# Lower triangles of 2,048 Gram matrices: four rows to a partition in place of two

## The chip, the cores and the metric

One NeuronCore of a Trainium2 chip runs the whole kernel. The metric is the device time of one execution in microseconds (us). The kernel before takes 437.03 us in the median of three runs (436.17 to 438.0).

## The reference

```python
B, N, D = (1024, 64, 256)          # the input really has 2048 of them
Z = jnp.einsum('bnd,bmd->bnm', inputs, inputs)
li, lj = jnp.tril_indices(64, k=-1)
return Z[:, li, lj]                # 2048 x 2016, float32
```

The input is 2048 x 64 x 256 in float32 (134 MB), the output 2048 x 2016 (16.5 MB). For each of the 2,048 batches all 64 rows are multiplied with each other, and what lies below the diagonal is stored row after row: row i has i values, so it begins at column i(i-1)/2.

## The kernel before, in words

**Tiles.** A tile is 16 batches: two *sides* of eight. There are 128 tiles. A matmul contracts over partitions, so the 256 numbers of a row must be brought onto partitions: they are cut into eight *chunks* of 32, and VectorE's transposition works on 32 x 32 blocks. A *slot* is one batch in each of the four quadrants of 32 partitions; each side has two slots.

**Load** (SP, L138). `x_pairs` (L62) joins two rows into a run of 512 numbers, 2,048 bytes. A side's DMA brings 256 such runs: partition p gets one run of slot 0 and one of slot 1. Two DMAs of 512 KB make a tile, into one of eight x_in slots (`IN_RING`); the load of tile t waits until tile t-8 has been turned, and those of tiles 2 to 4 until the tile before has landed (`APART`). After the load of every eighth tile SP issues the stores of a finished group (`store_whole`, L149, DMAs at L145), after waiting for its packing.

**First turn** (VectorE, L203). One instruction of 2,048 elements a partition turns all 32 x 32 blocks of a tile. A block has 32 partitions (32 row pairs, one batch) by 32 numbers; turned, it gives 32 partitions (numbers of a chunk) by 32 row pairs, which are written two elements apart, so that first and second rows of the pairs interleave and the 64 rows of a batch stand in order in x_turned. There are three such buffers (`LAP`); turn t waits for its load and for the matmuls of tile t-3.

**Matmuls** (TensorE, L256). For each slot, each chunk, each quadrant g and each side, the 32 x 64 piece of x_turned is both weights and moving side, so that 64 x 64 products add up over the eight chunks in PSUM. Eight array tiles (four quadrants by two sides) work side by side; each quadrant has a bank. The program is a loop over laps of three tiles. PSUM has two sets of four banks, with three slots each: a set fills in one and a half tiles. TensorE waits for `kept[1]` ahead of the first slot of set 1 and for `kept[0]` two chunks before the lap's end.

**Keep** (ScalarE, L282). Copies a full set from PSUM to `products`, which gathers a group of eight tiles (64 batches a side). Set 0's copy starts when half the lap is multiplied (`half_multiplied`), set 1's when the lap is.

**Row turn** (VectorE, L219). Per group four instructions (`PIECES`) of 1,024 elements turn products so that batches come onto partitions and the 64 columns j into the free dimension; the first is issued after turn t = 8 x group + 11, the others two tiles apart.

**Packing.** ScalarE copies rows to packed_rows (`pack`: L111 for short rows, L117 for pairs of long ones), in quarter pieces behind each keep; GpSimd carries the second halves of long rows across partitions (L122). Both wait until the store of the group two before has landed. The last group is shared with VectorE (L122) and GpSimd (L111).

The order on each engine is that of the program: SP the loads and stores, VectorE the turns with a row turn after every second one, ScalarE keep then packing.

Of the kernel before, what the change touches and what calls it, by code (L numbers as in the profile page):

```python
# [7 lines left out]
PARTS = 128  # L8
# [11 lines left out]
def gram_lower_triangle(nc: bass.Bass, x: bass.AP, y: bass.AP):  # L20
    BATCHES, ROWS, DIM = x.shape
    PACKED = y.shape[1]
    JOINED = ROWS // BLOCK
    CHUNKS = DIM // BLOCK
    SLOTS = 2
# [12 lines left out]
    SETS = 2  # L38
    SET_SLOTS = LAP * SLOTS // SETS
# [4 lines left out]
    GROUP_SLOTS = GROUP_TILES * SLOTS  # L44
# [16 lines left out]

    x_pairs = x.rearrange("b (i r) d -> (b i) (r d)", r=JOINED)  # L62

    with ExitStack() as stack:  # L64
# [5 lines left out]

        x_in = sbuf("x_in", [PARTS, IN_RING, SIDES * SLOTS, JOINED * DIM])
        x_turned = sbuf("x_turned", [PARTS, LAP, SIDES * SLOTS, CHUNKS, ROWS])
# [14 lines left out]
        half_multiplied = semaphore("half_multiplied")  # L87
# [9 lines left out]
        def place(t):  # L97

            return divmod(t + BLANK, LAP)

# [25 lines left out]
        def _(sync):  # L126
            def load(t):
# [67 lines left out]
        def _(dve):  # L195
            def turn(t):


                k, (lap, j) = t % IN_RING, place(t)
                dve.wait_ge(loaded[k], (t // IN_RING + 1) * (SIDES * 16))  # L200
                if lap > 0:
                    dve.wait_ge(tile_multiplied[j], lap * ARRAY_TILES)  # L202
                nc.vector.transpose(  # L203
                    x_turned[:, j].rearrange("p k c (i r) -> p k r c i", r=JOINED),
                    x_in[:, k].rearrange("p k (r c d) -> p k r c d", r=JOINED, c=CHUNKS)).then_inc(turned[j], LAP)

            def turn_rows(n):
                group, piece = divmod(n, PIECES)
                rows = piece_rows(piece)
                if piece == 0:  # L210

                    lap, s = divmod(((group + 1) * GROUP_SLOTS - 1 + BLANK * SLOTS) // SET_SLOTS, SETS)
                    dve.wait_ge(kept[s], (lap + 1 + s) * LAP)
                if group > 0:
# [5 lines left out]
                    row_halves[:, rows].rearrange("p i h j -> p (i h) j"),  # L220
# [20 lines left out]
        def _(pe):  # L241
            def multiply(j, step):

                pe.wait_ge(turned[j], step)
                for slot in range(SLOTS):
                    s, at = divmod(j * SLOTS + slot, SET_SLOTS)
                    if s == 1 and at == 0:
                        pe.wait_ge(kept[1], step)
                    for c in range(CHUNKS):
# [3 lines left out]
                        for g in range(QUADRANTS):  # L253
                            for side in range(SIDES):
                                rows = x_turned[g * BLOCK:(g + 1) * BLOCK, j, side * SLOTS + slot, c, :]
                                done = nc.tensor.matmul(  # L256
                                    bank_sets[s][side * HALF:(side + 1) * HALF, g, at, :], rows, rows,
                                    start=c == 0, stop=c == CHUNKS - 1)
                                if c == CHUNKS - 1:
                                    if slot == SLOTS - 1:  # L260
                                        done.then_inc(tile_multiplied[j], 1)
                                    elif at == SET_SLOTS - 1:
                                        done.then_inc(half_multiplied, 1)
# [6 lines left out]
        def _(act):  # L270
            def keep(lap, s):

                act.wait_ge(half_multiplied if s == 0 else tile_multiplied[LAP - 1], (lap + 1) * ARRAY_TILES)
                begin = (lap * SETS + s) * SET_SLOTS - BLANK * SLOTS
                slot, end = max(0, begin), begin + SET_SLOTS
                while slot < end:
                    group, in_group = divmod(slot, GROUP_SLOTS)
                    count = min(end - slot, GROUP_SLOTS - in_group)
                    if group >= KEPT_RING and in_group == 0:
# [3 lines left out]
                        products[:, group % KEPT_RING, :, in_group * QUADRANTS:(in_group + count) * QUADRANTS].rearrange(  # L283
# [47 lines left out]
```

## Time and profile before

| | |
|---|---|
| median of 3 runs | 437.03 us |
| profiled execution | 437.67 us, span 435.9 us |
| granted TensorE clock, mean | 0.975 |
| PE, PE weight loads | 88%, 87% of the span busy |
| DVE, ACT, POOL | 83%, 41%, 45% |
| load and store queue | 95.3% of 16 engines' span |
| HBM read, written | 134.22 MB, 16.52 MB, mean 346 GB/s |

The span runs from the first to the last instruction; the execution's own time is 1.8 us longer. PE is TensorE, DVE VectorE, ACT ScalarE, POOL GpSimd, SPq the queue of SyncE. Busy shares are means over the span. "issue" is time in which an engine waited for nothing that the profile shows. The granted clock is given as a share of 2.4 GHz, TensorE's upper level (the lower is 1.2 GHz).

### The profile page before, as it was taken

How to read it: one execution, taken by the hardware profiler on the slowest of the kernel's cores; microseconds unless marked ns; L12 is line 12 of the kernel's file. 1: busy time of each engine (PE TensorE's matmuls, PEld its weight loads, DVE VectorE, ACT ScalarE, POOL GpSimd, SP SyncE). 2: the span in 40 equal slices, each digit the busy share in tenths (PEclk: the TensorE clock that was granted, in tenths of full speed). 3: DMA queues.
4: the chain of work that ended last, by engine and by line, in shares of the span. 5: the costliest groups of instructions: out<-in, count | busy, mean ns of one | idle time of the engine just before them, and what ended most of it. 6: DMA issues, size and time to landing. Idle time of an engine off the chain costs nothing.

```text
span 435.9 us, 68822 instructions
## 1 busy us (share of the span) xinstructions
PE 385.4 (88%) x33024; PEld 377.5 (87%) x33024; DVE 363.7 (83%) x224; ACT 179.3 (41%) x834; POOL 197.2 (45%) x980
## 2 busy tenths in 40 slices
PE   4569999999999999999998999989899998989810
PEld 4569999999999999999998989989899998989810
DVE  5248899999999999897997979799697979979734
ACT  0101125454444535354444544533445454345372
POOL 0000082745628174471817446281744628173584
PEclk9999999999999999999999999999899999999965
DMA  5589999999999999999999999999999999999416
GB/s 199 192 312 388 387 387 387 387 391 392 387 398 386 402 387 368 369 394 357 356 398 344 390 377 387 353 352 378 373 384 368 379 365 373 361 386 368 107 34 156
DMA packets 72378, 151.01 MB, mean 346 GB/s; under 512 B 4640, under 2 KB 4768, under 8 KB 72352
## 3 DMA queue, kind: packets, MB, share of 16 engines
q1 hardware_dynamic: 72352, 150.75, 95.3%
q14 instruction: 20, 0.16, 0.1%
q8 instruction: 6, 0.10, 0.1%
HBM read 134.22 MB, written 16.52 MB: 346 GB/s over the span
## 4 chain that ended last, share of the span: by engine, by line
PE 35%; DMA 28%; DVE 16%; SPq 10%; issue 6%; POOL 3%; ACT 0%; DVEq 0%; POOLq 0%
PE bank_set L256 35%; DMA x_in<-x_dram 25%; DVE x_turned L203 12%; SPq L138 9%; DVE row_halves L219 3%; DMA y_dram<-packed_rows 3%; POOL packed_rows L122 3%; DVE packed_rows L122 1%; DVE x_turned L225 0%; SPq L145 0%; ACT packed_rows L117 0%; ACT products L282 0%; DVEq L202 0%; DVEq L218 0%; DVEq L64 0%
## 5 line engine op out<-in xcount | busy, mean ns | idle before, releaser
L256 PE MATMUL bank_set<-x_turned 32*64 32x64 f32 x33024 | 385.4, 237 | 30.0 <-issue 12.1
L256 PEld LDWEIGHTS bank_set<-x_turned 32*64 32x64 f32 x33024 | 377.5, 132 | 37.8 <-issue 21.9
L203 DVE STREAM_TRANSPOSE x_turned<-x_in 128x2048 f32<-128x2048 f32 x128 | 290.6, 2286 | 58.0 <-DMA x_in<-x_dram 41.5
L122 POOL COPY packed_rows<-row_halves 32x60 f32<-32x60 f32 (+30 forms) x961 | 194.9, 204 | 232.3 <-DMA y_dram<-packed_rows 132.5
L282 ACT COPY products<-bank_set 128x768 f32<-128x768 f32 (+2 forms) x96 | 69.0, 729 | 215.4 <-PE bank_set L256 204.9
L219 DVE STREAM_TRANSPOSE row_halves<-products 128x1024 f32<-128x1024 f32 x64 | 76.8, 1203 | 6.9 <-POOL packed_rows L122 5.0
L117 ACT COPY packed_rows<-row_halves 128x128 f32<-128x128 f32 x256 | 56.4, 300 | 17.4 <-DMA y_dram<-packed_rows 15.9
L111 ACT COPY packed_rows<-row_halves 128x32 f32<-128x32 f32 (+30 forms) x481 | 62.3, 220 | 0.0
L282 ACT ACT_TABLE_LOAD x1 | 1.3, 1283 | 15.8 <-PE bank_set L256 15.8
L122 DVE COPY packed_rows<-row_halves 32x2 f32<-32x2 f32 (+30 forms) x31 | 3.5, 191 | 0.0
L225 DVE MEMSET x_turned<- 128x2048 f32 x1 | 1.8, 1765 | 1.2 <-PEq L325 1.2
L111 POOL COPY packed_rows<-row_halves 128x2 f32<-128x2 f32 (+14 forms) x15 | 2.1, 195 | 0.1
L325 POOL MEMSET const-float32-0.0<- 128x1 f32 x1 | 0.1, 99 | 0.2 <-issue 0.2
L325 POOL MEMSET const-bfloat16-1.0<- 128x1 bf16 x1 | 0.1, 102 | 0.0
L325 POOL MEMSET const-uint8-127<- 128x1 uint8 x1 | 0.1, 102 | 0.0
L325 POOL MEMSET const-float32-1.0<- 128x1 f32 x1 | 0.1, 99 | 0.0
## 6 DMA issues: line engine op xcount, KB each, us to landing
x_in<-x_dram SPq DMA_DIRECT2D x256, 512.0 KB, 10.8
y_dram<-packed_rows SPq DMA_DIRECT2D x30, 504.0 KB, 9.6
y_dram<-packed_rows SPq DMA_DIRECT2D x2, 380.0 KB, 3.9
y_dram<-packed_rows SPq DMA_DIRECT2D x2, 124.0 KB, 3.9
```

Of the source, the lines that this page charges most:

```text
L111: return copy(packed_rows[:, group % 2, :, at:at + i], row_halves[:, i, :, 0:i])
L117: return copy(two[:, :, :, 0:BLOCK], row_halves[:, i:i + 2].rearrange("p w h j -> p h w j"))
L122: return copy(packed_rows[first:first + BLOCK, group % 2, :, at + BLOCK:at + i], row_halves[first + BLOCK:first + HALF, i, :, 0:i - BLOCK])
L138: sync.dma_start(x_in[:, k, side * SLOTS:(side + 1) * SLOTS], x_pairs[first:first + PER_SIDE * BLOCK].rearrange("(k p) e -> p k e", p=PART ...
L203: nc.vector.transpose(x_turned[:, j].rearrange("p k c (i r) -> p k r c i", r=JOINED), x_in[:, k].rearrange("p k (r c d) -> p k r c d", r=J ...
L219: nc.vector.transpose(row_halves[:, rows].rearrange("p i h j -> p (i h) j"), products[:, group % KEPT_RING, rows, :].rearrange("p i (h q) ...
L225: nc.vector.memset(x_turned[:, j], 0.0).then_inc(turned[j], LAP)
L256: done = nc.tensor.matmul(bank_sets[s][side * HALF:(side + 1) * HALF, g, at, :], rows, rows, start=c == 0, stop=c == CHUNKS - 1)
L282: last = nc.scalar.copy(products[:, group % KEPT_RING, :, in_group * QUADRANTS:(in_group + count) * QUADRANTS].rearrange("p i (m g) -> p i ...
L325: nc = bacc.Bacc("TRN2", target_bir_lowering=False, num_devices=1)
```

## The change

A run becomes four rows (1,024 numbers, 4,096 bytes), so a side's DMA is 128 runs, one per partition, and 32 partitions hold two batches of 16 runs. A row's number is 4i + r in run i; with i = 8h + n and r = 2u + v it is 32h + 4n + 2u + v. The first turn writes each turned block (32 columns: two batches of 16 runs) so that the rows of a batch stand in the order (h, u, n, v). The matmul takes this order as weights, so the products' partitions have it; on the moving side and in its output the columns are walked so that the products' columns come out in true order: the 64 results of a matmul go to PSUM in pairs of neighbours, four elements apart. The row turn puts the remaining order of the other index right: it writes pairs (v) of neighbours, four elements apart (n), for each u.

PSUM's two sets now hold two tiles and one tile: the keep of set 0 starts when the second tile of a lap is multiplied, and its copy has 1,024 elements, that of set 1 512. The copies' patterns get a dimension more (quadrant and slot change places). ScalarE's packing behind the two keeps is four and two quarter pieces a lap in place of three and three.

```diff
-    JOINED = ROWS // BLOCK
+    JOINED = 4
+    PAIR = 2
+    PAIRS = JOINED // PAIR
-    SLOTS = 2
+    SLOTS = BLOCK * JOINED // ROWS
-    SETS = 2
-    SET_SLOTS = LAP * SLOTS // SETS
+    SET_TILES = (2, 1)
+    SETS = len(SET_TILES)
...
-        x_in = sbuf("x_in", [PARTS, IN_RING, SIDES * SLOTS, JOINED * DIM])
-        x_turned = sbuf("x_turned", [PARTS, LAP, SIDES * SLOTS, CHUNKS, ROWS])
+        x_in = sbuf("x_in", [PARTS, IN_RING, SIDES, JOINED * DIM])
+        x_turned = sbuf("x_turned", [PARTS, LAP, SIDES, CHUNKS, SLOTS, ROWS])
...
+        def set_of(j):
+            return (0, j) if j < SET_TILES[0] else (1, j - SET_TILES[0])
...
-                    first = (group * GROUP + side * KEPT + in_group * PER_SIDE) * BLOCK
-                    sync.dma_start(x_in[:, k, side * SLOTS:(side + 1) * SLOTS],
-                                   x_pairs[first:first + PER_SIDE * BLOCK].rearrange("(k p) e -> p k e", p=PARTS)
-                                   ).then_inc(loaded[k], 16)
+                    first = (group * GROUP + side * KEPT) * (ROWS // JOINED) + in_group * PARTS
+                    sync.dma_start(x_in[:, k, side], x_joined[first:first + PARTS]).then_inc(loaded[k], 16)
...
                 nc.vector.transpose(
-                    x_turned[:, j].rearrange("p k c (i r) -> p k r c i", r=JOINED),
-                    x_in[:, k].rearrange("p k (r c d) -> p k r c d", r=JOINED, c=CHUNKS)).then_inc(turned[j], LAP)
+                    x_turned[:, j].rearrange("p s c b (h u n v) -> p u v (s c b h) n", h=ROWS // BLOCK, u=PAIRS, v=PAIR),
+                    x_in[:, k].rearrange("p s (u v e) -> p (u v) s e", u=PAIRS, v=PAIR)).then_inc(turned[j], LAP)
...
                 nc.vector.transpose(
-                    row_halves[:, rows].rearrange("p i h j -> p (i h) j"),
+                    row_halves[:, rows].rearrange("p i h (n u v) -> p (i h) u n v", u=PAIRS, v=PAIR),
...
-                                rows = x_turned[g * BLOCK:(g + 1) * BLOCK, j, side * SLOTS + slot, c, :]
+                                rows = x_turned[g * BLOCK:(g + 1) * BLOCK, j, side, c, slot]
                                 done = nc.tensor.matmul(
-                                    bank_sets[s][side * HALF:(side + 1) * HALF, g, at, :], rows, rows,
+                                    bank_sets[s][side * HALF:(side + 1) * HALF, g, at, :].rearrange(
+                                        "r (n u v) -> r u n v", u=PAIRS, v=PAIR),
+                                    rows,
+                                    rows.rearrange("d (h u e) -> d u h e", h=ROWS // BLOCK, u=PAIRS),
                                     start=c == 0, stop=c == CHUNKS - 1)
...
-                act.wait_ge(half_multiplied if s == 0 else tile_multiplied[LAP - 1], (lap + 1) * ARRAY_TILES)
+                j = SET_TILES[0] * s
+                act.wait_ge(tile_multiplied[j + SET_TILES[s] - 1], (lap + 1) * ARRAY_TILES)
...
-                        products[:, group % KEPT_RING, :, in_group * QUADRANTS:(in_group + count) * QUADRANTS].rearrange(
-                            "p i (m g) -> p i m g", g=QUADRANTS),
-                        bank_sets[s][:, :, slot - begin:slot - begin + count, :].rearrange("p g m i -> p i m g"))
+                        products[:, group % KEPT_RING, :, in_group * PER_SIDE:(in_group + count) * PER_SIDE].rearrange(
+                            "p i (m g b) -> p i m g b", g=QUADRANTS, b=SLOTS),
+                        bank_sets[s][:, :, (t - begin) * SLOTS:(t - begin + count) * SLOTS, :].rearrange(
+                            "p g (m b) i -> p i m g b", b=SLOTS))
...
-                    while n + PACK_LAG < (lap * SETS + s + 1) * SET_SLOTS - BLANK * SLOTS:
+                    while n + PACK_LAG < (lap * LAP + (SET_TILES[0] if s == 0 else LAP) - BLANK) * 2:
```

## Rows read from the trace of the kernel before

**Rows 1.** The page: span, busy time, load queue, bytes.

```profile
span 435.9 us, 68822 instructions
PE 385.4 (88%) x33024; PEld 377.5 (87%) x33024; DVE 363.7 (83%) x224; ACT 179.3 (41%) x834; POOL 197.2 (45%) x980
...
q1 hardware_dynamic: 72352, 150.75, 95.3%
...
HBM read 134.22 MB, written 16.52 MB: 346 GB/s over the span
```

**Rows 2.** The chain of waits in order of time: start us, us, what.

```profile
27.83 10.45 PE bank_set L256 x475
...
56.25 8.78 PE bank_set L256 x423
...
163.05 6.12 PE bank_set L256 x296
169.30 2.32 DVE x_turned L203
171.62 0.24 SPq L138
171.90 12.72 DMA x_in<-x_dram
```

**Rows 3.** Three stretches: length, busy us (instructions) of PE, PEld, DVE, ACT, POOL, clock, DMA, GB/s.

```profile
27.80:169.20 141.40, 139.52 (x12095) 137.52 (x12096) 128.83 (x67) 56.73 (x243) 63.35 (x310) 1.00 1.05 389
169.20:415.50 246.30, 232.93 (x20206) 227.98 (x20199) 215.66 (x117) 110.26 (x523) 120.73 (x589) 0.99 0.99 358
...
36.00:60.00 24.00, 23.59 (x2094) 23.20 (x2082) 20.53 (x11) 4.00 (x5) 4.97 (x24) 1.00 1.05 387
```

**Rows 4.** The waits: who for whom, us in total, times, longest us.

```profile
DVE x_turned L203 <- DMA x_in<-x_dram: 41.5, 15, 4.2
...
ACT packed_rows L117 <- DMA y_dram<-packed_rows: 15.9, 9, 3.6
```

**Rows 5.** The timeline of the end: start us, us, engine, line [idle before <- releaser].

```profile
407.54 20.07 POOL L122 COPY packed_rows<-row_halves 32x32 f32<-32x32 f32 x93 [10.22 <-DMA y_dram<-packed_rows]
...
412.50 2.95 PE L256 MATMUL bank_set<-x_turned 32*64 32x64 f32 x256 [1.05 <-DVE x_turned L203]
...
417.21 3.79 ACT L111 COPY packed_rows<-row_halves 128x32 f32<-128x32 f32 x31
...
422.81 3.50 DVE L219 STREAM_TRANSPOSE row_halves<-products 128x1024 f32<-128x1024 f32 x3 [5.01 <-POOL packed_rows L122]
...
426.34 3.49 DVE L122 COPY packed_rows<-row_halves 32x2 f32<-32x2 f32 x31
```

**Rows 6.** What the DMA engines moved, in 40 slices: 30 to 60 us, then 160 to 200.

```profile
GB/s 410 401 399 407 396 391 388 385 391 385 388 382 391 391 382 391 385 388 385 390 382 388 388 388 388 382 391 385 385 385 391 388 388 388 385 388 382 390 391 385
...
GB/s 391 381 383 391 377 387 391 383 414 401 352 314 307 350 307 295 356 377 397 401 408 389 381 371 373 365 391 395 389 383 385 391 387 385 449 408 319 239 334 358
```

**Rows 7.** Line 138, the issue of loads on SP: durations in ns, time to landing.

```profile
L138 SPq DMA_DIRECT2D x_in<-x_dram x256: 368/1229/3982, 0.7 to 397.3; - x128
...
DMA to landing us min/median/max: 3.3/10.8/15.2
```

**Rows 8.** Groups by form: count, busy us, mean ns, idle before by releaser.

```profile
L203 DVE STREAM_TRANSPOSE x_turned<-x_in 128x2048 f32<-128x2048 f32 x128 | 290.6, 2286 | 58.0 <-DMA x_in<-x_dram 41.5 <-PE bank_set L256 16.5
L219 DVE STREAM_TRANSPOSE row_halves<-products 128x1024 f32<-128x1024 f32 x64 | 76.8, 1203 | 6.9 <-POOL packed_rows L122 5.0 <-ACT products L282 1.9
L282 ACT COPY products<-bank_set 128x768 f32<-128x768 f32 x75 | 60.0, 800 | 185.1 <-PE bank_set L256 174.6 <-issue 10.4
...
L282 ACT COPY products<-bank_set 128x512 f32<-128x512 f32 x10 | 5.9, 589 | 18.1 <-PE bank_set L256 18.1
...
L111 ACT COPY packed_rows<-row_halves 128x32 f32<-128x32 f32 x16 | 3.6, 223 | 0.0
```

**Rows 9.** The timeline of the start, TensorE.

```profile
9.89 2.35 PE L256 MATMUL bank_set<-x_turned 32*64 32x64 f32 x128 [3.14 <-issue]
```

More of the change, by code:

```diff
@@ L59, in gram_lower_triangle @@
     STORES = SIDES * 16
-    x_pairs = x.rearrange("b (i r) d -> (b i) (r d)", r=JOINED)
+    x_joined = x.rearrange("b (i r) d -> (b i) (r d)", r=JOINED)
     with ExitStack() as stack:
@@ L210, in turn_rows @@
                 if piece == 0:
-                    lap, s = divmod(((group + 1) * GROUP_SLOTS - 1 + BLANK * SLOTS) // SET_SLOTS, SETS)
+                    lap, j = place((group + 1) * GROUP_TILES - 1)
+                    s = set_of(j)[0]
                     dve.wait_ge(kept[s], (lap + 1 + s) * LAP)
@@ L244, in multiply @@
                 pe.wait_ge(turned[j], step)
+                s, in_set = set_of(j)
+                if s == 1 and in_set == 0:
+                    pe.wait_ge(kept[1], step)
                 for slot in range(SLOTS):
-                    s, at = divmod(j * SLOTS + slot, SET_SLOTS)
-                    if s == 1 and at == 0:
-                        pe.wait_ge(kept[1], step)
+                    at = in_set * SLOTS + slot
                     for c in range(CHUNKS):
@@ L254, in multiply @@
                             for side in range(SIDES):
-                                rows = x_turned[g * BLOCK:(g + 1) * BLOCK, j, side * SLOTS + slot, c, :]
+                                rows = x_turned[g * BLOCK:(g + 1) * BLOCK, j, side, c, slot]
                                 done = nc.tensor.matmul(
-                                    bank_sets[s][side * HALF:(side + 1) * HALF, g, at, :], rows, rows,
+                                    bank_sets[s][side * HALF:(side + 1) * HALF, g, at, :].rearrange(
+                                        "r (n u v) -> r u n v", u=PAIRS, v=PAIR),
+                                    rows,
+                                    rows.rearrange("d (h u e) -> d u h e", h=ROWS // BLOCK, u=PAIRS),
                                     start=c == 0, stop=c == CHUNKS - 1)
[L259 to L263, printed above, removed]
+                                if c == CHUNKS - 1 and slot == SLOTS - 1:
+                                    done.then_inc(tile_multiplied[j], 1)
             with pe.Fori(LAP, (LAPS + 1) * LAP, LAP) as step:
@@ L271, in keep @@
             def keep(lap, s):
-                act.wait_ge(half_multiplied if s == 0 else tile_multiplied[LAP - 1], (lap + 1) * ARRAY_TILES)
[L274 to L278, printed above, removed]
+                j = SET_TILES[0] * s
+                act.wait_ge(tile_multiplied[j + SET_TILES[s] - 1], (lap + 1) * ARRAY_TILES)
+                begin = lap * LAP + j - BLANK
+                t, end = max(0, begin), begin + SET_TILES[s]
+                while t < end:
+                    group, in_group = divmod(t, GROUP_TILES)
+                    count = min(end - t, GROUP_TILES - in_group)
                     if group >= KEPT_RING and in_group == 0:
```

4 lines of the change are left out of this document (1 added, 3 removed).

## The prediction

> **What bounds the kernel now.** I read the page first: a span of 435.9 us in an execution of 437.67 us, TensorE busy for 88% of it, VectorE for 83%, the load queue for 95% [rows 1]. Three resources are near full, so the averages decide nothing and the stage does. The chain in order of time shows two stages [rows 2]. From 56.25 to 163.05 us it is TensorE alone, twelve laps of three tiles in 106.8 us, 8.90 us a lap or 2.967 us a tile. From 169.3 us on it goes through the load, the issue of loads on SP and the first turn (L203). The split by stretch says the same [rows 3]: up to 169.2 us TensorE is busy 139.5 of 141.4 us, after it 232.9 of 246.3 us, with 13.4 us idle. The waits name the giver: L203 waited 41.5 us for loads [rows 4]. So two thirds of the kernel wait for loads that come a little too slowly.
>
> How much too slowly: TensorE's second lap starts at 27.83 us [rows 2] with 126 tiles to go. By 169.2 us it has done 141.4 / 2.967 = 47.6 of them; the other 78.4 take until 415.45 us [rows 5], 3.14 us each. A tile's loads are 512 packets of 2,048 bytes, 1.049 MB, at the 387 GB/s of the stretch without stores 2.71 us [rows 3]; the other 0.43 us are the share of stores (0.13 MB a tile) and hold-ups. The queue thus falls behind by 3.14 - 2.967 = 0.173 us a tile from the start, and what it had in hand (eight x_in slots) covers 47.6 x 0.173 = 8.2 us. Check: 126 x 0.173 - 8.2 = 13.6 us, the idle time seen.
>
> **The change part by part.**
>
> *Loads.* The 134.22 MB read [rows 1] come in runs of 2,048 bytes, 65,536 packets; now in 32,768 of 4,096; bytes, DMAs (256) and their order stay. The trace has no load in 4,096-byte packets. Lower bound of the gain: none, 2.71 us a tile. Upper bound: the best slice of the trace, 449 GB/s in the stretch from 160 us, where a store lies beside loads: 2.34 us. I take the row nearest to a pure load at its best, the first four slices after 30 us (410, 401, 399, 407 GB/s, mean 404) [rows 6]: 2.60 us. Then a tile costs the queue 3.03 us, the lag is 0.063 us a tile, 126 x 0.063 = 7.9 us, inside the 8.2 us in hand: TensorE never waits. So 13.6 us go. A rate of 404 GB/s is also the point from which they go entirely; at 395 GB/s (2.65 us) 126 x 0.113 - 8.2 = 6.0 us would stay.
>
> A load stream in rows of 4 KiB issued from SP is given 408.7 GB/s in the Trainium skill (DMA: Bandwidth & Descriptors, iDMA fabric). By it a tile's loads would cost 2.57 us and the sum would be the same; no run here shows it yet.
>
> *Issues on SP.* A load's issue lasts 1.2 us in the median and lands 10.8 us later, 256 packets each [rows 7]: SP is held back by a full queue, with some eight DMAs out. With half the packets it can run further ahead, until x_in slots hold it. The store sits behind the load of the same tile as before. SP then comes to a store some tiles earlier and may wait there for ScalarE's packing with loads behind it; that is hidden by what is already queued, and without that cover costs the same lag as above. No direct term.
>
> *First turn (L203).* 128 instructions of 2,048 elements, before 2.286 us [rows 8], output in steps of 8 bytes over runs of 32; now in steps of 8 bytes over runs of 8, then a jump. *Row turn (L219).* 64 instructions of 1,024 elements at 1.203 us with an output without steps; now pairs of elements 16 bytes apart. The two rows differ by 1.08 us for 1,024 elements, 1.06 ns each, and L219 alone is at 1.17 with its fixed part: the 8-byte step costs nothing today. I take both unchanged. Bounds: nothing, or the price of a stall at each jump, which no row shows; what can be said is the room: 2.286 + 1.203 / 2 = 2.89 us a tile against 2.967, or 2.7%. Up to that it is hidden by TensorE.
>
> *Matmuls.* Their number stays, 33,024. The weights are read as before; the moving side reads runs of 16 elements, and the 64 results land in pairs of 8 bytes, 16 bytes apart. Eight array tiles run side by side, so each takes a weight load and a matmul in 2.967 / 32 = 92.7 ns. Lower bound: nothing changes; upper: one cycle of the 2.4 GHz level (granted clock 1.00) lost at each of 32 pairs, 13 ns, 14%. I take nothing, as nearest to the only row there is, L203's steps being free on its own port.
>
> The rule that speaks against this part is in the Trainium skill (PSUM — Partial Sum Buffer, Specifications): PSUM lines are of 8 bytes, and "any non-contiguous AP slows matmuls significantly". Advanced Engine Details and Errata, Memory Cachelines, is milder: every two consecutive elements should be contiguous, which pairs keep. By the first the third rival below comes true; by the second the sum stands. The trace cannot say, since every output in it is contiguous.
>
> *Keeps on ScalarE (L282).* Before, two copies of 768 elements a lap, 0.800 us each; now one of 1,024 and one of 512. By the forms of 512 and 768 at 0.589 and 0.800 us [rows 8] the first is 1.01 us: 1.60 us a lap both ways. What moves is the due time. The set of two tiles is free for reading after two thirds of a lap instead of half, and TensorE asks for it at 14/16 of the third tile: 14/16 x 2.967 = 2.60 us for a copy of 1.01 us, 1.3 us to spare with the start delay. Behind a keep ScalarE packs: now four quarter pieces after the large one and two after the small (three and three before). Four short ones are 16 copies of 0.22 us, 3.5 us [rows 8]: with the keep 4.5 us after two thirds of the lap, so that the small keep starts 1.5 us late, but TensorE needs its set only two thirds of a lap (5.9 us) on. Two are 1.8 us, done long before the large keep is due. Its waits for stores came to 15.9 us in nine [rows 4]; one of over 4 us after the small keep would reach TensorE. The longest was 3.6 us, so no cost.
>
> *Head.* Up to 27.83 us TensorE works in chunks of 128 matmuls with gaps that no engine releases, as the 3.14 us before the one at 9.89 us [rows 9]; the loads of tiles 2 to 4 are still issued one by one. Unchanged; 1 us either way.
>
> *Tail.* Today the last matmul ends at 412.50 + 2.95 = 415.45 us and the span 20.45 us later. In it, the last group's row turns wait 5.0 us for GpSimd at 422.81 us: its 62 carries of the group before start only at 407.54 us, after 10.22 us of waiting for a store that lands behind queued loads [rows 5]. With loads ahead of TensorE that store lands well before and this wait goes. Next in line is ScalarE, which must free the rows: 31 short copies ended at 421.0 us, 5.55 us after the last matmul. From there one row turn (1.2 us), VectorE's 31 carries (3.49 us) and the final stores (429.83 to 435.9, 6.1 us): 16.3 us. If the store lands no earlier than the last load must (393 us), GpSimd ends at 408.5 and the tail is some 19.7 us.
>
> **Sum.** 27.83 + 126 x 2.967 (373.8) = 401.7 us for the last matmul, + 16.3 = 418.0 us of span, + 1.8 us around it = 419.8 us, against 437.67 us. The median of the runs before, 437.03, lies 0.6 us under the profiled one, so I predict 419.5 us, 4% less.
>
> **The rivals.**
> 1. *A packet of 4,096 bytes moves no faster* (or is cut in two by the queue, so the change does nothing). For: the rate rests at 387 GB/s for 24 us with all engines at work, whatever the packet's fixed part. Then 13.6 us of idle time and the old tail stay: 437 us. Between this and the forecast lie 388 to 404 GB/s, 425 to 434 us.
> 2. *VectorE becomes the bound.* Its turns would have to lengthen by over 2.7% to show, and by (13.6 + 4.1) / 126 = 0.14 us a tile more, so 7.5%, to eat the whole gain. At 15%, 2.89 becomes 3.32 us a tile: 27.8 + 418.6 + 16.3 + 1.8 = 464 us. Against: steps of 8 bytes are free in L203's row.
> 3. *The matmuls slow down at their results' pairs.* TensorE is the very engine that is left as the bound, so each per cent costs 3.7 us; break-even at 17.7 / 373.8 = 4.7%. At one cycle a pair, 3.38 us a tile: 27.8 + 426 + 16.3 + 1.8 = 472 us. For: nothing in the trace has such an output. Against: moving and writing go on in other array tiles meanwhile.
>
> **How the numbers follow.** Forecast (414 to 425 us) 0.60; part of the loads' wait stays (425 to 434) 0.13; rival 1, 0.09; rival 2, 0.06; rival 3, 0.12. A measurement of this kernel can tell some 0.5% from no change. So faster 0.73, same 0.09, slower 0.18. The range runs from 414 us (head and tail each somewhat shorter) to 437 us, rival 1's own time, leaving rivals 2 and 3 out.
>
> **What would show it.** Right: load packets 32,768 and the queue at 400 GB/s or more in the steady stretch; laps of 8.90 us up to the last one; L203 waiting for TensorE, not for loads; L203 at 2.28 us, L219 at 1.20 us; the large keep at 1.01 us; the last matmul near 402 us and no wait for GpSimd in the tail. Wrong: a lap above 9.0 us with TensorE busy throughout (rival 3, matmul rows longer), VectorE at 9 tenths everywhere with TensorE waiting for it and no load wait (rival 2), 387 GB/s again (rival 1).

## The result and the profile after

The changed kernel takes 429.87 us in the median of four runs (429.42 to 430.58), the kernel before 437.45 us beside it: ratio 0.983, 95% interval 0.981 to 0.985. It is faster, by 1.7%, where 4% were forecast (419.5 us), and it stands inside the stated range, 414 to 437 us.

The page of the profiled execution (430.24 us), to be laid beside [rows 1]:

```profile
span 428.5 us, 68861 instructions
PE 379.3 (89%) x33024; PEld 372.2 (87%) x33024; DVE 365.0 (85%) x224; ACT 177.9 (42%) x829; POOL 197.3 (46%) x980
...
DMA packets 39610, 151.01 MB, mean 352 GB/s; under 512 B 4640, under 2 KB 4768, under 8 KB 39584
...
q1 hardware_dynamic: 39584, 150.75, 92.8%
```

The 32,768 packets fewer are there, and TensorE is busy for 6.1 us less. That already is a surprise, since its instructions are as many as before. The chain in order of time shows three stages (start us, us, what):

```profile
21.90 4.22 issue
26.12 2.27 PE bank_set L264 x114
28.39 4.47 issue
32.86 10.62 PE bank_set L264 x512
...
61.28 8.66 PE bank_set L264 x431
...
316.42 8.67 PE bank_set L264 x433
...
331.33 1.01 ACT products L291
...
382.52 17.53 DMA y_dram<-packed_rows
400.10 0.20 POOL packed_rows L130
```

TensorE's second lap starts at 32.86 us, 5.03 us later than in [rows 2]. From 61.28 to 316.42 us lie 29 laps, 8.80 us each against 8.90. From 331 us on it waits for loads again, and a store of 17.53 us leads into the tail. The timeline gives the end (start us, us, engine, line, last the idle time before and who ended it):

```profile
400.10 20.07 POOL L130 COPY packed_rows<-row_halves 32x32 f32<-32x32 f32 x93 [9.41 <-DMA y_dram<-packed_rows]
...
404.99 2.95 PE L264 MATMUL bank_set<-x_turned 32*64 32x64 f32 x256 [0.73 <-DVE x_turned L208]
...
415.37 3.50 DVE L225 STREAM_TRANSPOSE row_halves<-products 128x1024 f32<-128x1024 f32 x3 [5.29 <-POOL packed_rows L130]
```

The last matmul ends at 407.94 us and the span 20.6 us after it, the same tail as in [rows 5]: GpSimd starts its last 62 carries when the store lands, and the last group's row turns wait for it for 5.29 us. The groups by form answer to [rows 8]:

```profile
L208 DVE STREAM_TRANSPOSE x_turned<-x_in 128x2048 f32<-128x2048 f32 x128 | 292.0, 2290 | 49.2 <-PE bank_set L264 29.5 <-DMA x_in<-x_dram 18.7
L225 DVE STREAM_TRANSPOSE row_halves<-products 128x1024 f32<-128x1024 f32 x64 | 76.9, 1205 | 6.9 <-POOL packed_rows L130 5.3 <-ACT products L291 1.6
...
L291 ACT COPY products<-bank_set 128x1024 f32<-128x1024 f32 x37 | 37.5, 1012 | 164.2 <-PE bank_set L264 146.2 <-issue 18.0
L291 ACT COPY products<-bank_set 128x512 f32<-128x512 f32 x54 | 31.1, 586 | 47.7 <-PE bank_set L264 46.3 <-issue 1.1
```

The new patterns cost VectorE nothing to speak of: 2,290 ns against 2,286, and 1,205 against 1,203. The large keep takes 1,012 ns.

**Where the time went.** I split each span into the same parts: start of the second lap, 42 laps at the steady rate, what TensorE waits beyond that, and the tail after the last matmul. The third term is a remainder. It holds more than waits for loads: the second lap is longer than the steady ones in every kernel, by 1.7 us before (27.83 to 38.41 us) and by 2.0 us after (32.86 to 43.70 us). That leaves 12.1 and 3.6 us for loads that come late.

| us | second lap | 42 laps (one) | waits | last matmul ends | tail | span |
|---|---|---|---|---|---|---|
| before | 27.8 | 373.8 (8.90) | 13.8 | 415.4 | 20.5 | 435.9 |
| forecast | 27.8 | 373.8 (8.90) | 0 | 401.7 | 16.3 | 418.0 |
| after | 32.9 | 369.5 (8.80) | 5.6 | 407.9 | 20.6 | 428.5 |

Between the two kernels the span falls by 7.4 us: 8.2 us of waits and 4.3 us of laps are won, 5.0 us of head are lost. The forecast missed by 10.5 us: +5.0 in the head, -4.3 in the laps, +5.6 in the waits, +4.3 in the tail.

### The profile page after: what moved, and what is told of

Its sections match the earlier page's. It is cut to its first block, busy times and chain, and to the rows that moved or that the text cites. A ratio compares the mean times of both kernels' runs of the same rounds, so it can differ in the third digit from the quotient of the medians.

```text
span 428.5 us, 68861 instructions
## 1 busy us (share of the span) xinstructions
PE 379.3 (89%) x33024; PEld 372.2 (87%) x33024; DVE 365.0 (85%) x224; ACT 177.9 (42%) x829; POOL 197.3 (46%) x980
## 4 chain that ended last, share of the span: by engine, by line
PE 72%; SPq 11%; issue 6%; DMA 4%; POOL 3%; DVE 2%; ACT 0%; DVEq 0%; POOLq 0%; ACTq 0%
PE bank_set L264 72%; SPq L146 10%; DMA y_dram<-packed_rows 4%; POOL packed_rows L130 3%; SPq L151 1%; DVE packed_rows L130 1%; DVE row_halves L225 1%; DVE x_turned L231 0%; ACT products L291 0%; ACT packed_rows L125 0%; DVEq L67 0%; SPq L157 0%; DVEq L224 0%; POOLq L187 0%; ACTq L282 0%
## 5 line engine op out<-in xcount | busy, mean ns | idle before, releaser
L264 PE MATMUL bank_set<-x_turned 32*64 32x64 f32 x33024 | 379.3, 236 | 28.7 <-issue 18.2
L264 PEld LDWEIGHTS bank_set<-x_turned 32*64 32x64 f32 x33024 | 372.2, 132 | 35.6 <-issue 28.1
L208 DVE STREAM_TRANSPOSE x_turned<-x_in 128x2048 f32<-128x2048 f32 x128 | 292.0, 2290 | 49.2 <-PE bank_set L264 29.5
L291 ACT COPY products<-bank_set 128x512 f32<-128x512 f32 (+1 forms) x91 | 68.6, 759 | 211.9 <-PE bank_set L264 192.5
L225 DVE STREAM_TRANSPOSE row_halves<-products 128x1024 f32<-128x1024 f32 x64 | 76.9, 1205 | 6.9 <-POOL packed_rows L130 5.3
L291 ACT ACT_TABLE_LOAD x1 | 1.3, 1283 | 20.6 <-PE bank_set L264 20.6
```

The lines of the kernel that those rows point to most:

```text
L208: nc.vector.transpose(x_turned[:, j].rearrange("p s c b (h u n v) -> p u v (s c b h) n", h=ROWS // BLOCK, u=PAIRS, v=PAIR), x_in[:, k].rea ...
L225: nc.vector.transpose(row_halves[:, rows].rearrange("p i h (n u v) -> p (i h) u n v", u=PAIRS, v=PAIR), products[:, group % KEPT_RING, row ...
L264: done = nc.tensor.matmul(bank_sets[s][side * HALF:(side + 1) * HALF, g, at, :].rearrange("r (n u v) -> r u n v", u=PAIRS, v=PAIR), rows, ...
L291: last = nc.scalar.copy(products[:, group % KEPT_RING, :, in_group * PER_SIDE:(in_group + count) * PER_SIDE].rearrange("p i (m g b) -> p i ...
```

## The experiments

"Second lap", "waits" and "tail" are the parts of the table above, read from the one execution of each kernel that was traced, and totals are medians of two to ten executions. The runs before beside the experiments lie at 436.8 to 437.2 us.

### The sets alone, on the kernel before

```diff
# on the kernel before
-    SET_SLOTS = LAP * SLOTS // SETS
+    SET_TILES = (2, 1)
...
-                                if c == CHUNKS - 1:
-                                    if slot == SLOTS - 1:
-                                        done.then_inc(tile_multiplied[j], 1)
-                                    elif at == SET_SLOTS - 1:
-                                        done.then_inc(half_multiplied, 1)
+                                if c == CHUNKS - 1 and slot == SLOTS - 1:
+                                    done.then_inc(tile_multiplied[j], 1)
```

(with ScalarE's trigger, its packing and the waits of TensorE as in the change; two-row loads and all patterns stay)

> The kernel before with PSUM sets of two tiles and one tile and nothing else of the change: two-row loads, one increment-group (half_multiplied) gone, no wait inside a tile. Theory (the lap fell from 8.90 to 8.79 us because the accounting of the sets changed, not the patterns): steady laps of 8.79 us, head and packets as before, the waits for loads begin a little earlier since TensorE asks sooner, so the time falls by 0 to 2 us only. Rival (the lap fell because of the new patterns of operands or results): laps stay at 8.90 us and the time is that of before within 0.3%.

Measured: 436.95 us, ratio 1.001 (0.999 to 1.003). The chain in order of time of this kernel:

```profile
28.93 3.93 issue
32.87 10.31 PE bank_set L260 x489
...
43.31 8.64 PE bank_set L260 x430
51.95 0.12 issue
52.08 8.65 PE bank_set L260 x426
```

Laps of 8.77 us: the shorter lap belongs to the sets, not to the new patterns. The patterns themselves cost at most 0.03 us a lap, and probably nothing, since the kernels with small stores and with stores from ScalarE (below) have the new patterns and laps of 8.77 us too. What I had not expected is the first number: the second lap starts at 32.87 us, as in the changed kernel, with packets of 2,048 bytes. So the head's 5 us do not need the larger packets. My expectation of the head "as before" was wrong. The two cancel: 42 x 0.13 = 5.5 us gained, 5.0 lost.

This run is also the clean partner of the changed kernel: same sets, same head (32.87 and 32.86 us), two DMAs a tile in both. What differs is the row layout with its packets of 4,096 bytes: 436.95 against 429.87 us, 7.1 us. They come out of the waits: 12.9 us here (last matmul at 414.19 us), 5.6 after; without the longer second lap 11.2 and 3.6 us.

### Eight increments a lap put back

```diff
# on the changed kernel
                                 if c == CHUNKS - 1 and slot == SLOTS - 1:
                                     done.then_inc(tile_multiplied[j], 1)
+                                elif c == CHUNKS - 1 and j == 1:
+                                    done.then_inc(half_multiplied, 1)
```

> The changed kernel with eight more semaphore increments a lap on the last matmuls of the first slot of the second tile, which nobody waits for. Theory (the lap fell by 0.11 to 0.13 us with the sets because eight increments a lap went with them): laps of 8.90 us again, 4.6 us more in all up to where loads bound. Rival (it fell because TensorE's wait for the second set no longer stands inside a tile): laps stay at 8.79 us.

Measured: 430.21 us (427.54 to 432.55), 0.3 us more than the changed kernel, where up to 4.6 us were expected. The execution traced is the slowest, 432.55 us. The timeline of TensorE shows nine laps in 80.29 us:

```profile
124.11 80.12 PE L265 MATMUL bank_set<-x_turned 32*64 32x64 f32 x6912 [0.17 <-issue]
204.39 80.12 PE L265 MATMUL bank_set<-x_turned 32*64 32x64 f32 x6912 [0.17 <-issue]
```

8.92 us a lap: an increment on a matmul costs TensorE some 15 ns. Against the changed kernel's trace (430.24 us) 42 x 0.12 = 5.0 us are lost in the laps, and 2.7 are given back, since the waits fall from 5.6 to 2.9 us as TensorE comes later. That is the 2.3 us between the two traced executions; the medians differ by less, within the 5 us over which this kernel's four runs scatter.

### Two increments a tile in place of eight

On the kernel with stores from ScalarE and spaced loads (below), only the last quadrant's two matmuls tell that a tile is done.

```diff
-    ARRAY_TILES = QUADRANTS * SIDES
+    ARRAY_TILES = SIDES
...
-                                if c == CHUNKS - 1 and slot == SLOTS - 1:
+                                if c == CHUNKS - 1 and slot == SLOTS - 1 and g == QUADRANTS - 1:
```

> The kernel with stores from ScalarE's queue and spaced loads, and only the matmuls of the last quadrant (two in place of eight) telling that a tile is done, so 6 increments a lap in place of 24. The run with 8 more increments had laps of 8.91 us against 8.79, so 15 to 16 ns each. Theory (each increment costs TensorE its 15 ns): 18 fewer take 0.27 us off a lap, 8.50 us. The loads then bound: the queue's 24.7 us a group of eight tiles is 3.09 us a tile against 2.83, so TensorE waits from the middle on and the total falls by 0 to 3 us only, 416.5 to 420 us. Rival (only the increments inside a tile cost, those at a tile's end lie beside a wait): laps stay at 8.77 us.

Measured: 420.17 us, no gain on its base (419.5). The laps fell from the base's 8.77 to 8.50 us as computed, 11.3 us in all, and the second lap starts 1.1 us sooner, at 28.76 us. The waits took all of it: 16.8 us against 3.8. At this point the loads are the bound, and a faster TensorE gains nothing.

### Packets of 2,048 bytes in the changed kernel, and four DMAs in the kernel before

```diff
# on the changed kernel; the waits for a tile's loads count 32 a side in place of 16
-                    sync.dma_start(x_in[:, k, side], x_joined[first:first + PARTS]).then_inc(loaded[k], 16)
+                    for half in range(2):
+                        part = slice(half * 2 * DIM, (half + 1) * 2 * DIM)
+                        sync.dma_start(x_in[:, k, side, part], x_joined[first:first + PARTS, part]).then_inc(
+                            loaded[k], 16)
```

> The changed kernel with each load cut in two along the run, so that all packets are of 2,048 bytes again (four DMAs of 256 KB a tile) while turns, matmuls and sets stay changed. Theory (the packets give the queue its rate, and their number in the queue sets both the run-ahead of SP and the head): queue at 387 GB/s, packet 84 ns, TensorE's second lap starts near 28 us as before instead of 32.9, laps of 8.79 us while fed, waits for loads from some 160 us on, total 435 to 438 us. Rival A (the head comes from the order and spacing of the loads, not from the packets): second lap still starts at 32 to 33 us and the total is 440 us or more. Rival B (the gain is TensorE's shorter lap alone): total stays at 430 us.

Measured: 443.81 us, ratio 1.016 (1.011 to 1.020), slower than the kernel before. The second lap starts at 29.9 us. Neither expectation fits: the total is above the theory's 435 to 438 us, and the head is shorter than rival A's 32 to 33 us. The edit also doubles the DMAs, so a second run does that alone, on the kernel with the sets alone:

```diff
-                    sync.dma_start(x_in[:, k, side * SLOTS:(side + 1) * SLOTS],
-                                   x_pairs[first:first + PER_SIDE * BLOCK].rearrange("(k p) e -> p k e", p=PARTS)
-                                   ).then_inc(loaded[k], 16)
+                    for slot in range(SLOTS):
+                        at = first + slot * PARTS
+                        sync.dma_start(x_in[:, k, side * SLOTS + slot], x_pairs[at:at + PARTS]).then_inc(loaded[k], 16)
```

> The kernel before with sets of two tiles and one (two-row loads) and each load cut by slot into two DMAs of 128 packets: four DMAs of 256 KB a tile, packets of 2,048 bytes, as in the run of the changed kernel with packets of 2,048 bytes. It tells how much of that run's 443.8 us is the number of DMAs. Theory (half is the packets, half the DMAs): 440 to 444 us, as there. Rival (the number of DMAs costs nothing, the packets all): 437 us, as with two DMAs a tile.

Measured: 441.48 us, 4.5 us over the two-DMA kernel. Four DMAs of 256 KB a tile are dearer than two of 512 KB with the same packets. The 2.3 us by which the changed kernel so cut (443.81 us) still lies above this one are not explained. Two views say what the packets do. DMA, 36 to 60 us, of the changed kernel cut to 2,048 bytes, then of the changed kernel with spaced loads (below), which streams undisturbed there:

```profile
DMA packets 5093, 9.29 MB, mean 387 GB/s; under 512 B 566, under 2 KB 566, under 8 KB 5092
```

```profile
DMA packets 2712, 9.89 MB, mean 412 GB/s; under 512 B 300, under 2 KB 300, under 8 KB 2711
```

The larger packet is worth 6% of the rate; it gives more than the 404 GB/s that I had taken. The Trainium skill's 408.7 GB/s for rows of 4 KiB (DMA: Bandwidth & Descriptors, iDMA fabric) agrees with the 412 within 1%. While TensorE bounds, the changed kernel itself shows no such rate (380 GB/s from 36 to 60 us): SP waits there for free x_in slots.

### More loads spaced

```diff
# on the changed kernel, and likewise on the kernel before with the sets alone
-    APART = range(2, 5)
+    APART = range(2, 7)
```

> The changed kernel with the loads of tiles 2 to 6 issued one by one instead of tiles 2 to 4. Theory (the two gaps of 4.2 and 4.5 us in TensorE's first lap are fetches of its program that stand behind loads which now run further ahead): the gaps fall to 2.2 to 3 us, the second lap starts at 28.5 to 30 us, but the waits for loads of the end stay or grow, since two loads come later; total 427 to 429.5 us. Rival (the gaps come from the size of the packets alone): second lap at 32.9 us again and a total at or above 430 us.

> The kernel before with sets of two tiles and one and the loads of tiles 2 to 6 issued one by one, packets of 2,048 bytes. Theory (the head's delay of 5 us belongs to the moment at which the unspaced loads are released, not to the packet size): second lap at 29 to 30 us instead of 32.9 us; the total stays within 1.5 us of 437 us, since loads bound from the second half on. Rival: head unchanged.

Measured: the changed kernel falls to 426.0 us (0.977, 0.972 to 0.982), 1 us below the range that I gave, since the waits did not grow (4.7 us). The kernel before with the sets alone rises to 439.85 us, a miss: I had it within 1.5 us of 437. The changed kernel's chain now reads

```profile
25.03 2.27 PE bank_set L264 x115
27.31 2.28 issue
29.59 10.16 PE bank_set L264 x475
```

The gaps of 4.2 and 4.5 us are 2.6 and 2.3 us, and the second lap starts at 29.59 us. In the other kernel it starts at 27.93 us, 4.9 us earlier, and the total is 2.9 us worse. The reason is in the waits, 21.4 us against 12.9: with spaced loads the DMA engines move 252 GB/s from 30 to 36 us in place of 393 and 209 in place of 265 before that, and TensorE waits for loads from 115 us on. I read this as the queue's idle time in the head, which a kernel that the queue bounds does not get back.

What decides the head? TensorE runs 128 matmuls, then waits with no engine to release it; the instruction queue of the page has six packets, 0.10 MB, one for each 128 of a lap's 768 matmuls. SP's own waits show when the free loads are let go. Where three loads are spaced, the sum of SP's waits for them and the start of the second lap are: before 16.8 us and 27.8; stores from ScalarE 15.8 and 28.5, on the kernel before 15.8 and 30.3; packets cut 14.7 and 29.9; more increments 14.2 and 32.9; sets alone 14.1 and 32.9; small stores 13.8 and 32.3; after 13.6 and 32.9. Longer waits of SP mostly go with an earlier second lap, but the sets alone with four DMAs break the rule: 12.1 and 28.8. The two views of SP's waits, before and after:

```profile
SPq L138 <- DMA x_in<-x_dram: 16.8, 3, 6.6
```

```profile
SPq L146 <- DMA x_in<-x_dram: 13.6, 3, 6.0
```

In the changed kernel the flood of unspaced loads starts 3 us earlier, and two gaps are over 4 us where the kernel before has none. I read this as fetches of TensorE's program that stand beside the loads. That the fetch is what TensorE waits for is inferred. The granted clock is no rival: it is 0.66 in the first 30 us of the kernel with the sets alone and 1.00 in the kernels before and after, and the steps of 128 matmuls take 2.25 to 2.36 us in all three. Why the sets let the spaced loads land sooner stays open. So does whether it is the sets: moving the stores to ScalarE changes no instruction of this stretch on SP or TensorE, and it shortens the changed kernel's head by 4.4 us and lengthens that of the kernel before by 2.5. The head shifts by several us with edits elsewhere.

### Small stores

```diff
# on the changed kernel
             def store_whole(group):
...
-                store(group, slice(0, PACKED))
+                store(group, slice(0, 128))
```

This leaves out columns 128 to 2,015 of the output of all groups but the last.

> The changed kernel with the stores of all groups but the last cut to their first 128 columns; the other columns of these groups are left out of the output. Theory (stores cost the queue 4.3 us a group, by holding some engines back, and that is why TensorE waits for loads from 331 us on and why the last store lands 17.5 us after its issue): no wait of TensorE for the first turn after the head, the last matmul at 32.9 + 42 x 8.79 = 402 us, GpSimd's wait in the tail gone, total 418 to 421 us. Rival (loads alone at 412 GB/s with eight slots are late): waits stay and the total is above 425 us.

Measured: 420.1 us in the median of two runs; last matmul at 402.28 us, tail 15.7 us. TensorE waits for no turn after the head; the waits' whole list for L208 is

```profile
DVE x_turned L208 <- PE bank_set L264: 31.7, 47, 10.2
...
DVE x_turned L208 <- DMA x_in<-x_dram: 5.9, 3, 2.4
```

So the loads of the changed kernel are late because of the stores, and so is the tail. In the stretch where loads bound, eight tiles of the changed kernel take 24.8 and 24.6 us (the same matmul of three successive groups starts at 355.62, 380.41 and 404.99 us). Its loads need 8 x 1.049 MB / 412 GB/s = 20.4 us, which leaves 4.3 us for two stores; I had carried over 8 x 0.43 = 3.4 us.

### Stores from ScalarE's queue

```diff
# on the changed kernel; SP keeps the stores of the last two groups
             def pack(n):
...
                 if quarter == 3:
                     last.then_inc(packed_home, 1)
+                if piece == 0 and quarter == 3 and 0 < group < GROUPS - 1:
+                    done = group - 1
+                    act.wait_ge(packed_home, (done + 1) * PIECES)
+                    act.wait_ge(packed_across, (done + 1) * LONG_PIECES)
+                    for side in range(SIDES):
+                        first_row = done * GROUP + side * KEPT
+                        nc.scalar.dma_start(y[first_row:first_row + KEPT, :].rearrange("(h q) c -> q h c", q=BLOCK),
+                                            packed_rows[side * HALF:side * HALF + BLOCK, done % 2, :, :]).then_inc(
+                            stored[done % 2], 16)
```

> The changed kernel with the stores of groups 0 to 13 issued from ScalarE's queue instead of SP's, each after the first long quarter pieces of the next group. Theory (the tail is long because the store of group 12 stands behind loads in SP's queue: 17.5 us from issue to landing, so GpSimd begins its last 62 carries only at 400.1 us; the loads are late because stores take engine time, whatever queue they come from): a store lands in under 9 us, GpSimd's and ScalarE's waits for stores shrink, the part after the last matmul falls from 20.6 to 16 to 17 us, while the waits of the first turn for loads stay within 2 us of those of the changed kernel (18.7 us); total 424 to 427 us. Rival (the stores delay by standing in line, not by engine time): the waits for loads vanish too, total at or below 421 us.

Measured: 419.84 us, 0.961 (0.959 to 0.964) of the kernel before and 10 us under the changed kernel. The total is below the first theory's 424 to 427 us and in the rival's range (at or below 421); the parts decide between them. The timeline of GpSimd at the end:

```profile
388.08 15.27 POOL L130 COPY packed_rows<-row_halves 32x32 f32<-32x32 f32 x62 [8.95 <-DVE row_halves L221]
405.34 5.13 POOL L130 COPY packed_rows<-row_halves 32x32 f32<-32x32 f32 x31 [1.99 <-DMA y_dram<-packed_rows]
```

The last 62 carries start at 388.08 us, released by VectorE's row turn and no longer by a store. The tail is 15.3 us. That store was issued at 372.62 us in place of 381.48, and no store from ScalarE took over 9.4 us to land, against 18.5 from SP: it is issued sooner as well as landing sooner, and these runs do not part the two. The waits stay at 5.2 us, so the mechanism is the first theory's: they do not vanish with the stores out of SP's queue. Of the 11.3 us that the span is shorter, 5.3 are the tail, 4.4 the head, 28.48 us here, which neither theory had, 1.2 the laps (8.77 us) and 0.4 the waits. The two together,

> Both together: stores from ScalarE's queue and the loads of tiles 2 to 6 issued one by one. If the two gains are independent: head as in the run with spaced loads (second lap at 29.6 us), tail of 16 to 17 us, total 420 to 423 us. Rival (an earlier TensorE meets the same late loads, so the head's gain is lost to them): total as with the stores alone.

give 419.5 us (0.961, 0.958 to 0.964): second lap 29.85 us, waits 3.8, last matmul 401.86 us against 401.92 with the stores alone. The rival holds: by then the head no longer counts. Against the changed kernel with spaced loads alone (426.0 us), whose head is within 0.3 us of this one's, moving the stores is worth 6.5 us, 5.2 of them in the tail; the waits fall by 0.9 us only. And on the kernel before, with its own sets and packets:

> The kernel before with the stores of groups 0 to 13 issued from ScalarE's queue. Theory (the tail's 4 to 5 us are a matter of the store's place behind loads, in both kernels): the part after the last matmul falls from 20.5 to 15.5 to 16.5 us, the waits for loads stay, total 431 to 434 us. Rival (the shorter tail needs the faster loads): 436 to 438 us.

432.01 us (0.990, 0.986 to 0.993), tail 16.1 us. The store's place in SP's queue cost both kernels over 4 us.

### What holds the queue back at the end

DMA of the changed kernel with stores from ScalarE and spaced loads, 376 to 402 us in 40 slices; its last loads are in it:

```profile
DMA  9999999999930000000000000000000000000999
GB/s 426 399 449 381 418 412 409 403 410 410 372 126 25 25 25 25 32 25 25 25 25 25 32 25 25 25 25 13 0 0 0 0 0 0 0 0 0 198 198 198
```

For some 10 us the queue moves 25 GB/s, a sixteenth of its rate. I read this as one DMA engine still at work when fifteen are done, with the last load landing when it is. With small stores this stretch is missing. Three runs on this base ask what puts it behind.

```diff
# stores by half: 32 packets a DMA in place of 64, two DMAs for one
+                        for h in range(RUNS):
+                            at = done * GROUP + side * KEPT + h * BLOCK
+                            nc.scalar.dma_start(y[at:at + BLOCK, :],
+                                                packed_rows[side * HALF:side * HALF + BLOCK, done % 2, h, :]).then_inc(
+                                stored[done % 2], 16)
# more instructions on SP, after each load from tile 8 on
+                    for extra in range(20):
+                        sync.wait_ge(turned[extra % LAP], 1)
# more instructions on GpSimd, after each piece of groups 0 to 12
+                        for extra in range(80):
+                            pool.wait_ge(turned[extra % LAP], 1)
```

> The kernel with stores from ScalarE's queue and spaced loads, each store cut into its two halves of 32 batches: 32 packets of 8,064 bytes a DMA in place of 64. In the run before this cut, one DMA engine alone was still at work (25 GB/s) for some 10 us after the others had emptied their last loads. Theory S (the stores' spread over the engines or their clash there puts that engine behind): the lone engine's stretch changes by over 3 us either way and the total with it. Theory F (it also carries the instruction fetches, 0.26 MB, which at 25 GB/s are 10 us): the stretch stays at 9 to 11 us, total 419 to 422 us, more DMAs costing 0 to 2 us.

> The same base with 2,400 more instructions on SP that wait for nothing (semaphores long reached), some 150 KB of program at 64 bytes each, or about 19 fetches of 8 KB. Theory F (one engine carries all fetches and each load's landing waits for it): the lone engine's stretch at the end grows from 10 us to 14 to 17 us, TensorE's waits for loads begin earlier and grow, total 3 to 6 us more than 419.5. Theory S: stretch 9 to 11 us, total 419 to 421 us.

> The run with more instructions on SP became 7 us longer, but SP also issues the loads. Here some 1,040 empty instructions (80 waits a piece, merged in pairs) stand on GpSimd instead, behind its carries of groups 0 to 12, where it has 9 us a group to spare and issues no load. Theory F (fetches delay the loads): some 8 fetches more, TensorE's waits for the first turn grow from 3.8 to 8 or 9 us, total 423 to 426 us. Rival (the run on SP was longer because SP issued its loads later): waits as in the base, total 419 to 421 us.

Stores by half: 421.62 us and the same lone stretch. Halving the stores' packets a DMA does not matter. More instructions on SP: 427.35 us, waits 9.9 us, above the 3 to 6 us more that were forecast; on GpSimd: 421.04 us, waits 5.3 us against 3.8, not the 8 or 9 forecast. The page counts the fetches of the run on GpSimd:

```profile
q14 instruction: 29, 0.24, 0.1%
q8 instruction: 6, 0.10, 0.1%
```

Eight fetches of 8 KB more than its base's 21 cost 1.5 us, inside the scatter of the runs (419.7 to 422.5 against 417.8 to 422.6). The run on SP got less than it was meant to: the 2,400 waits became 1,200 instructions and 9 fetches more, not 19. What tests the theory of the fetches best is the lone stretch. At 25 GB/s nine more fetches would lengthen it by some 3 us (an estimate from these counts), but 25 GB/s last 9 to 10 us in the two kernels with more fetches as in their base. I therefore read most of what the run on SP lost as SP's own delay in issuing loads, which no run shows by itself. That a sixteenth of the queue ends late is shown, and that without the stores' bytes it does not. The two runs with more fetches speak against the fetches, and what in the stores does it stays open.

## Why the prediction was right or wrong

**Direction, bound and main cause held.** The gain of the row layout comes, as the prediction had it, from TensorE's waits for loads: 12.9 us fall to 5.6 between the two kernels that differ in it alone. Turns, matmul patterns and keeps cost what was taken: 2,290 and 1,205 ns, at most 0.03 us a lap, 1,012 ns. It is luck that the total misses by no more than 10.5 us: the laps, which I had as unchanged, gave 4.3 us that hide as much of the three other misses. Rival 1 fell (412 GB/s), rival 2 fell, and rival 3 with it: results in pairs of 8 bytes do not slow a matmul down. On the Trainium skill's two sentences (PSUM — Partial Sum Buffer, Specifications, and Advanced Engine Details and Errata, Memory Cachelines), this trace agrees with the milder one for pairs, though the section that has it repeats the strict one beside it; no run here has other patterns.

**"Then a tile costs the queue 3.03 us ... TensorE never waits"** failed. The rate term was too low (412 against 404 GB/s, 2.55 us a tile), but the term for stores and hold-ups was 0.54 us a tile, not the 0.43 carried over: 3.09 us. And TensorE asked sooner, every 2.93 us. By 331 us the lag of 0.16 us a tile had used up what was in hand, and 3.6 us of waits for loads stayed.

The account of what was in hand was wrong too, and there it was luck that the miss is not larger: 126 x 0.16 - 8.2 would be 12 us of waits. The lag does not run "from the start". The first stores are issued at 90.0 us before and 91.6 us after, and until then a tile costs the queue 2.71 and 2.55 us, less than TensorE's 2.97 and 2.93. Nor is the reserve fixed at 8.2 us; it depends on how far the queue gets ahead before the stores begin. SP's waits for a free x_in slot over the whole run, before and after, show it:

```profile
SPq L138 <- DVE x_turned L203: 21.7, 20, 2.0
```

```profile
SPq L146 <- DVE x_turned L208: 133.7, 70, 8.8
```

Between 36 and 100 us the kernel before has none of them and the changed kernel 50.4 us: its slots are full when the stores begin. From 91.6 to 331 us TensorE takes 82 tiles, and 82 x 0.16 = 13 us were used up, not 8.2. From 331 us on 25 tiles are left, and 25 x 0.16 = 4.0 us fits the 3.6 measured.

The mistake in kind: I took the remainder of a load-bound stretch as a constant price of stores (0.43 us), and it was 0.54 with the larger packets. It may hold the late engine's lag as well, which a larger load packet need not shorten; that is argued and no run shows it.

**"Head. ... Unchanged; 1 us either way"** failed by 5.0 us. I had looked at the change's loads and not at the moment when the free ones start, nor at how easily this stretch moves. The sets alone bring the same 5 us in their trace, and an edit of the stores that touches nothing here takes 4.4 of them away again. The cause stays open.

**"With loads ahead of TensorE that store lands well before and this wait goes"** failed by 4.3 us. The loads were not ahead at the end, and the store of group 12 took 17.5 us to land. The bound that I gave for this, a tail of 19.7 us, was near (20.6). With the store out of SP's queue the tail is 15.3 us, a little under the 16.3 us of the sum.

**The lap was taken as fixed** at 8.90 us; it fell to 8.80. Eight of 32 increments a lap go with `half_multiplied`, which the diff shows, and I gave them no term. They come to 8 x 15 ns x 42 = 5 us.

## What to carry to other kernels

When three resources are within 7% of each other, a change to one is worth what the next leaves over, so write down each one's period over the same unit (here 2.93, 3.09 and 2.89 us a tile for TensorE, queue and VectorE) before pricing anything. Put a store that others wait for on a queue without loads in front of it: in the tail that alone was worth over 4 us in both kernels, more than half of what the larger packets brought. Judge a change by the same kernel with only its side edits in: here the kernel with the side edit gained 5.5 us in the laps, had a head 5.0 us longer, and showed nothing in the total. And before a shift of a few us at the start of a kernel is laid to an edit, see whether an edit elsewhere shifts it too.

## What the runs showed of the hardware

- A semaphore increment on a matmul costs TensorE about 15 ns when it is the bound: laps of 8.92 and 8.80 us with 32 and 24 increments, and of 8.77 and 8.50 us with 24 and 6.
- Load packets of 4,096 bytes move at 409 to 412 GB/s, of 2,048 at 387; splitting a tile's two DMAs into four with the same packets cost 4.5 us over 128 tiles.
- After the last loads the queue moves 25 GB/s, a sixteenth of its rate, for 9 to 10 us in the six variants of the changed kernel with stores from ScalarE: one of 16 DMA engines, as I read it, that far behind the rest. The mean busy share from 160 to 300 us (1.01 to 1.02) does not show it. With the stores cut to 128 columns the stretch is missing.
- The first lap of a loop on TensorE goes in steps of 128 matmuls with gaps of 1.1 to 4.8 us; the second lap started anywhere from 27.8 to 32.9 us, and by 2.5 to 4.4 us differently between kernels that have the same instructions on SP and TensorE up to there.
